# A mixer's decays: read as repeated rows and clamped by ScalarE, in place of products on TensorE

## The reference

```python
proj = einsum('bld,pd->blp', hidden_states, in_proj_w)
gate, hbc, dt = proj[..., :I], proj[..., I:I + CONV_DIM], proj[..., -H:]
xBC = silu(conv_bias + sum_k pad(hbc)[:, k:k + L, :] * conv_weight[:, k])
x, Bm, Cm = xBC[..., :I], xBC[..., I:I + GN], xBC[..., I + GN:]
dt_p = softplus(dt + dt_bias);  A = -exp(A_log);  dA = exp(dt_p * A)
# step over the tokens, per head:
state = state * dA_t + dtx_t * B_t;  y_t = state . C_t
y = y + x * D;  yn = (y * rsqrt(mean_group(y * y) + EPS)) * norm_weight * silu(gate)
out = einsum('bli,di->bld', yn, out_proj_w)
```

## Time and profile before

| what | value |
|---|---|
| median of 3 runs | 1298.97 us (1296.31 to 1299.89) |
| the profiled execution | 1300.67 us |
| its span | 1298.9 us |
| TensorE busy (PE) | 1230.5 us, 95% |
| VectorE busy (DVE) | 933.9 us, 72% |
| ScalarE busy (ACT) | 702.5 us, 54% |
| GpSimd busy (POOL) | 653.6 us, 50% |
| moved by DMA | 57.52 MB, mean 44 GB/s |

### The profile page before, as it was taken

The page is one execution under the profiler, slowest core; times in us unless marked ns, Lnnn a source line. Parts: engine busy times, 40 slices in busy tenths (PEclk is TensorE's granted clock), DMA queues, the critical chain, the costliest instruction groups (busy, mean ns, idle before and its releaser), DMA issues. The chain is left out here.

```text
span 1298.9 us, 22009 instructions
## 1 busy us (share of the span) xinstructions
PE 1230.5 (95%) x6680; PEld 968.9 (75%) x6690; DVE 933.9 (72%) x1735; ACT 702.5 (54%) x1056; POOL 653.6 (50%) x707
## 2 busy tenths in 40 slices
PE   5999999999999999999999999999679999889976
PEld 4777777787778778777778878777557777667754
DVE  5786778669667866966886696688567555479995
ACT  3676676567567666756766675665543333222210
POOL 5057546655655655565465556545653343433330
PEclk9999999999999999999999999999789999889996
DMA  5111021011102101110210110010103322211100
GB/s 178 46 50 34 2 67 34 19 34 49 33 1 66 33 17 33 50 32 1 66 32 17 33 58 24 5 34 2 41 17 115 97 90 83 93 49 48 45 16 25
DMA packets 44233, 57.52 MB, mean 44 GB/s; under 512 B 10117, under 2 KB 21159, under 8 KB 43929
## 3 DMA queue, kind: packets, MB, share of 16 engines
q1 hardware_dynamic: 44185, 56.92, 14.3%
HBM read 49.95 MB, written 6.96 MB: 44 GB/s over the span
## 5 line engine op out<-in xcount | busy, mean ns | idle before, releaser
L722 DVE SCALAR_TENSOR_TENSOR conv<-p_tile,conv_taps,conv 128x511 f32<-128x511 f32 x189 | 141.3, 748 | 51.4 <-ACT conv L583 36.4
L831 DVE TENSOR_TENSOR em<-em,p_gb 128x512 f32<-128x512 f32 x128 | 82.1, 683 | 69.6 <-ACT em L630 69.5
L527 POOL TENSOR_TENSOR squares<-squares 128x256 f32<-128x256 f32 x64 | 48.0, 750 | 132.5 <-ACT squares L656 132.5
L94 PE MATMUL p_tile<-xn_hi,wc_hi 128*128 128x512 f32 x252 | 110.8, 440 | 0.9 <-DVE halo L726 0.9
L656 ACT ACTIVATE squares<-y 128x512 f32<-128x512 f32 x64 | 40.4, 631 | 112.5 <-DVE y L867 111.5
L722 DVE SCALAR_TENSOR_TENSOR conv<-p_gate,conv_taps,conv 128x511 f32<-128x511 f32 (+2 forms) x90 | 67.0, 745 | 46.7 <-ACT conv L583 43.1
L94 PE MATMUL p_tile<-xn_lo,wc_hi 128*128 128x512 f32 x252 | 98.8, 392 | 0.0
L94 PE MATMUL p_d<-wr_hi,zt_hi 128*128 128x512 f32 x236 | 94.0, 398 | 1.5 <-ACT em L630 1.5
L94 PE MATMUL p_d<-wr_lo,zt_hi 128*128 128x512 f32 x236 | 93.1, 394 | 0.0
L495 POOL TENSOR_TENSOR x_w<-xs,head_g 128x512 f32<-128x512 f32 x56 | 58.4, 1043 | 68.7 <-ACT xs L624 63.6
L588 ACT ACTIVATE xbc<-conv 128x512 f32<-128x512 f32 x96 | 60.7, 632 | 59.7 <-DVE conv L730 37.4
(11 more groups left out here) (393 smaller groups left out, 3605.1 us busy)
## 6 DMA issues: line engine op xcount, KB each, us to landing
w_raw<-w SPq DMA_DIRECT2D x108, 256.0 KB, 2.7
q_words<-q SPq DMA_DIRECT2D x33, 256.0 KB, 2.7
h_ring<-h_lo_rows SPq DMA_DIRECT2D x6, 704.0 KB, 4.8
h_lo_rows<-h_rest SPq DMA_DIRECT2D x11, 256.0 KB, 2.1
x_res<-x SPq DMA_DIRECT2D x8, 256.0 KB, 4.1
out<-out_t SPq DMA_DIRECT2D x8, 256.0 KB, 2.0
h_lo_rows<-h_rest SPq DMA_DIRECT2D x11, 128.0 KB, 1.9
gate_second<-w SPq DMA_DIRECT2D x4, 256.0 KB, 5.0
```

The lines of the kernel that those rows point to most:

```text
L94: pe.matmul(out, lhs(k)[0], rhs(k)[n], start=(start and k == 0 and n == 0), stop=False)
L722: ve.scalar_tensor_tensor(out=conv[:, s, sh:], in0=p[:, 0:HALF - sh], scalar=conv_w[:, bass.ds(g, 1), j, tap], in1=conv[:, s, sh:], op0=AL ...
L831: ve.tensor_tensor(m, m, gm.unsqueeze(1).broadcast_to([P, HG // 2, P]), ALU.mult)\
```

## The change

TensorE's products L1085 and L1095 go, with the bf16 parts of cum, `d_lhs`, `d_rhs`, `head_rows` and their DMAs. In their place the start writes cum and exp(cum) to DRAM in float32, [chunk, head, token]. Per chunk one DMA reads the group's 8 rows of cum, 1024 columns, into all 128 partitions of em (`load_cum`), and two DMAs read each head's row of exp(cum) into that head's 64 partitions of e_cum (`load_e_cum`). ScalarE then makes relu(cum[s] - cum[t]) in place, per head, with cum[s] as a bias column from `cum_tok` (`decay_steps`, 8 activations of 128x128), and later exp of minus that; the clamp takes the mask's place, and the product with B and C stays masked. The exp of e_cum is done once, at the start.

```diff
+        def load_cum(g, c):
+            n = g * NC + c
+            wait(sp, s_intra, n - 1)
+            row = at(sp, g + c * G)
+            sp.dma_start(em[:, c % 2, :], cum_rows.rearrange("c (g h) t -> (c g) (h t)", g=G)[bass.ds(row, 1), :]
+                         .broadcast_to([P, HG * P])).then_inc(s_dl[c % 2], 16)
+        def load_e_cum(g, c):
+            wait(sp, s_t, g * (NC - 1) + c - 1)
+            row = at(sp, g + c * G)
+            own = e_rows.rearrange("c (g j a) t -> (c g) a j t", g=G, a=2)[bass.ds(row, 1)]
+            for a in range(2):
+                sp.dma_start(by_tile(e_cum[a * HD:(a + 1) * HD, :]),
+                             own[:, a, :, :].broadcast_to([HD, GW // P, P])).then_inc(s_ecl, 16)
...
         def group(g, last):
             for c in range(NC):
+                if c + 1 < NC:
+                    load_e_cum(g, c + 1)
                 if c + 2 < NC:
-                    load_d(g, c + 2)
+                    load_cum(g, c + 2)
...
+        def decay_steps(g, c):
+            act.wait_ge(s_dl[c % 2], 16 * (g * (NC // 2) + c // 2 + 1))
+            for h in range(HG):
+                steps = em[:, c % 2, h * P:(h + 1) * P]
+                made = act.activation(steps, steps, ACT.Relu, scale=-1.0, bias=cum_tok[:, c, bass.ds(g * HG + h, 1)])
+            made.then_inc(s_e, 1)
...
-                act.wait_ge(s_d, n + 1)
-                wait(act, s_intra, n - 1)
-                if last and c >= CH:
-                    act.activation(e_cum[:], p_in[:], ACT.Exp).then_inc(s_ec, 1)
-                for k, p in enumerate((p_d0, p_d1)):
-                    act.activation(em[:, c % 2, k * 512:(k + 1) * 512], p[:], ACT.Exp).then_inc(s_e, 1)
-                if c > 0 and not (last and c >= CH):
-                    act.activation(e_cum[:], p_in[:], ACT.Exp).then_inc(s_ec, 1)
+                act.wait_ge(s_e, 3 * n + 1)
+                for k in range(2):
+                    decay = em[:, c % 2, k * 512:(k + 1) * 512]
+                    act.activation(decay, decay, ACT.Exp, scale=-1.0).then_inc(s_e, 1)
...
+                if c < NC - 1:
+                    decay_steps(g, c + 1)
+                elif not last:
+                    decay_steps(g + 1, 0)
                 act.wait_ge(s_y, n + 1)
...
+        act.wait_ge(ln_st, NC + 3)
+        act.activation(t_ecum, t_cum, ACT.Exp).then_inc(dt_ac, 1)
         act.wait_ge(dt_tp, 3)
         act.activation(by_half(dtw_t), transposed(p_gb), ACT.Exp).then_inc(dt_ac, 1)
-        act.activation(by_half(etot_t), transposed(p_d0), ACT.Exp).then_inc(dt_ac, 1)
+        act.wait_ge(dt_tp, 4)
+        act.activation(by_half(etot_t), transposed(p_y), ACT.Exp).then_inc(dt_ac, 1)
...
                     wait(ve, s_sq, n)
                     wait(ve, s_z, n)
+                    ve.wait_ge(s_ecl, 32 * st)
                     ve.tensor_tensor(y[:], p_in[:], e_cum[:], ALU.mult).then_inc(s_t, 1)
...
-                pe.wait_ge(s_dl[c % 2], 32 * (g * (NC // 2) + c // 2 + 1))
-                if c > 0:
-                    wait(pe, s_t, g * (NC - 1) + c - 1)
-                    for j in range(GW // P):
-                        pe.matmul(p_in[:, j * P:(j + 1) * P], head_rows[:, j, :], d_lhs[:, c % 2, :],
-                                  start=True, stop=True)
-                wait(pe, s_e, 2 * n)
-                wait(pe, s_res, n - 2 if tail and c > CH else n - 1)
-                wait(pe, s_v, n - 1)
...
-                for k in rows_in(last, c - 1):
-                    pe.wait_ge(l2_lo, k + 1)
-                for k, p in enumerate((p_d0, p_d1)):
-                    mm = pe.matmul(p[:], d_lhs[:, c % 2, :], d_rhs[:, c % 2, k * 512:(k + 1) * 512],
-                                   start=True, stop=True)
-                mm.then_inc(s_d, 1)
...
                 if not first and not tail:
-                    pe.wait_ge(s_e, 2 * n + 1)
                     out_product(n - 1, out_bank(last, c))
-                    pe.wait_ge(s_e, 2 * (n + 1))
+                    wait(pe, s_v, n - 1)
                     sum_rows(n - 1, ss_bank(last, c))
...
             conv_tile(j, 0, j, 0, (p_tile, p_d1)[j % 2])
+            if j == 2:
+                pe.wait_ge(dt_ve, 12)
+                for b in range(CH):
+                    mm = pe.transpose(p_y[:, b * P:(b + 1) * P],
+                                      t_cum[:, (b + 1) * P - 1:(b + 1) * P].broadcast_to([P, P]), ident[:])
+                mm.then_inc(dt_tp, 1)
```

More of the change, by code:

```diff
@@ L172, in mixer @@
     gm = p_gb[:, 2 * P:3 * P]
[L176 removed]
+    cum_rows, e_rows = (nc.dram_tensor(k, [NC, H, P], F32, kind="Internal").ap() for k in ("cum_rows", "e_cum_rows"))
     w_rows = io["w"].rearrange("n p c -> (n p) c")
@@ L192, in mixer @@
         sem(f"l2_{k}") for k in ("st", "var", "rs", "xn", "tr", "hi", "lo"))
[L194 to L198, removed]
+    s_xt, s_gb, s_prj, s_gate, s_ss, s_out, s_inter, s_intra, s_stn = (
+        sem(f"pe_{k}") for k in ("xt", "gb", "prj", "gate", "ss", "out", "inter", "intra", "stn"))
+    s_xs, s_e, s_cin, s_xc, s_sg, s_zhi, s_sq, s_whi = (
+        sem(f"act_{k}") for k in ("xs", "e", "cin", "xc", "sg", "zhi", "sq", "whi"))
     s_head = sem("ve_head")
@@ L339, in mixer @@
     t_w = y[:]
-    t_parts = [x[:, 0:GW // 2].bitcast(BF16) for x in (x_dt, x_w, x_d)]
+    t_ecum = x_d[:]
     t_mask = squares[:, 0:GW // 2].bitcast(BF16)
@@ L398, in sync @@
             load_w(0, w)
-        for k in range(PART):
-            wait(sp, dt_ve, 12 + k)
+        for rows, made in ((cum_rows, (ln_st, NC + 3)), (e_rows, (dt_ac, 6))):
+            sp.wait_ge(*made)
             for a in range(2):
[L403 to L408, removed]
+                heads_a = (t_cum if rows is cum_rows else t_ecum)[a * H:(a + 1) * H, :]
+                sp.dma_start(rows[a * CH:(a + 1) * CH].rearrange("c h t -> h c t"),
+                             heads_a.rearrange("h (c t) -> h c t", t=P)).then_inc(s_parts, 16)
+        sp.wait_ge(s_parts, 16 * 4)
+        load_cum(0, 0)
+        sp.wait_ge(dt_tp, 4)
+        sp.wait_ge(dt_ve, 11)
+        load_cum(0, 1)
         def group(g, last):
             for c in range(NC):
+                if c + 1 < NC:
+                    load_e_cum(g, c + 1)
                 if c + 2 < NC:
-                    load_d(g, c + 2)
+                    load_cum(g, c + 2)
                 elif not last:
-                    load_d(g + 1, c + 2 - NC)
+                    load_cum(g + 1, c + 2 - NC)
                 if not last:
@@ L1038, in row_transpose @@
             if p_row[k] is p_d1:
-                pe.wait_ge(s_e, 2 * (n + 1))
+                wait(pe, l2_lo, {2: 1}.get(k, 0))
                 if k == NC - 2:
@@ L1110, in group @@
                     pe.wait_ge(s_stu, g * (NC - 1) + c)
-                    pe.wait_ge(s_ec, g * (NC - 1) + c)
+                    wait(pe, s_t, g * (NC - 1) + c - 1)
                     for j in range(GW // P):
@@ L1165, in tensor @@
         pe.wait_ge(dt_ve, 11)
-        for src, dst in ((t_dt, p_y), (t_rem, p_gb), (None, p_d0)):
+        for src, dst in ((t_dt, p_y), (t_rem, p_gb), (t_cum, p_d0)):
             for b in range(CH):
-                rows_c = src[:, b * P:(b + 1) * P] if src is not None \
-                    else t_cum[:, (b + 1) * P - 1:(b + 1) * P].broadcast_to([P, P])
-                mm = pe.transpose(dst[:, b * P:(b + 1) * P], rows_c, ident[:])
+                mm = pe.transpose(dst[:, b * P:(b + 1) * P], src[:, b * P:(b + 1) * P], ident[:])
             mm.then_inc(dt_tp, 1)
```

68 lines of the change are left out of this document (14 added, 54 removed).

## The result

| | before | the changed kernel |
|---|---|---|
| median | 1298.97 us | 1290.65 us (1289.21 to 1294.09, 5 runs) |
| ratio | | 0.9942, 95% interval 0.992 to 0.9965 |
| profiled execution, its span | 1300.67, 1298.9 | 1290.2, 1288.3 |
| PE / ACT busy | 1230.5 / 702.5 us | 1199.4 / 822.0 us |
| moved by DMA | 57.52 MB | 105.01 MB |

The account below looks back on a forecast made before the run. TensorE's own work was taken to set seven of eight groups. From 1300.67 us: -28.0 for seven groups, -1.6 and -5.0 in the last, +3.2 start, -1.7 from profile to median: 1268 us, range 1256 to 1289.

Parts of the forecast that it names:

- VectorE's work stays: VectorE in the loop: its 128 products with em and the taps remain; y times e_cum now waits for a DMA.
- The clamp's price: ScalarE, eight clamps per chunk: 0.30 us each from start to start, 2.4 us per chunk, bounds 0.2 and 0.39.
- Rival 1: ScalarE's clamps don't overlap, 0.39 us each, 0.72 us more per chunk: 1285 us in all; chance 0.17.
- Rival 3: The em loads come late, over 12.3 us each, so ScalarE waits at the clamps: slower than before; chance 0.08.
- rival 4: No change: the removed products fill time TensorE would wait anyhow, the start eats the rest: 1297 to 1301; chance 0.05.
- Chunk 0 to 1: Loop boundary where the clamps delay squares and the rounded z holds out_product: gives nothing, -0.1 us.
- Chunk 1 to 2: Loop boundary where the convolution tile waits 0.1 us for the gate's silu, clamps hidden: 0.56 us won.
- 0.2 to spare: Chunk 1 to 2, ScalarE: clamps and squares end at 543.2, ahead of the gate's silu at 543.39.
- Chunks 4 to 5 and 5 to 6: Loop boundaries where the convolution tile waits for the gate's silu to empty p_tile: 0.56 us won each.
- Chunks 2 to 3, 3 to 4, 6 to 7 and 7 to 0: Loop boundaries: the first three, with the bank free early, give 0.66 us each; 7 to 0 gives 0.44.
- The start: Before the loop: later exp of chunk totals +2.9, first clamps +1.5, out_product's em wait gives back 1.2; together +3.2 us.
- The tail: Last group, chunks 4 to 7: waits for p_d's bank and e_cum go; 5.0 us won, between 2 and 9.

Follow-up runs that it names:

- best2: Changed kernel, e_cum wait on TensorE, ScalarE's loop written out, chunk 1's clamps behind z's rounding, start's exp behind the tiles' copies: 1268.6 us, 0.9758.
- dve_unrolled: The changed kernel with VectorE's hardware loop over groups 1 to 6 written out, ScalarE's loop kept: 1281.53 us, ratio 0.9883.
- before_pad12: The kernel before with twelve unused one-column activations a chunk added on ScalarE in chunks 1 to 7 of the looped groups: 1299.81 us, 1.0003.

## Why the prediction was wrong

The terms of the sum come to -31.4 us, and -10.6 was measured in the profiled executions (spans 1298.9 and 1288.3). Term by term:

| term | forecast | measured |
|---|---|---|
| start (first heads' product 69.85 to 75.67, then 1.25 won at 0-1) | +3.2 | +4.6 |
| seven group ends and boundaries, jumps aside | -28.0 | -21.8 |
| jumps back, five | none | +12.1 |
| last group, to chunk 3 | -1.6 | -0.2 |
| last group, chunks 3 to 7 | -5.0 | -3.3 |
| behind it | 0 | -1.9 |

**The step that failed** is a missing one, the largest part of the 20.8 us between the two: the jump back stood in the sum at nothing, without a reason. The part on ScalarE priced each added instruction by its time on the engine, but nothing asked what longer bodies do to the loop's jump. "VectorE's work stays" was true of its work; the seven register instructions a turn that came with its new wait were not counted, and with them taken off VectorE its stall of 5.4 to 6.1 us is gone. In place of nothing the runs showed 12.1 us over five jumps. The second part is the term of the boundaries, 6.2 us too large, taken up below. With the jumps cured, the kernel runs at 1279 to 1280 us, inside the range though 11 to 12 above the forecast.

**The clamp's price was right.** A row of eight lasts 2.44 us, (2.44-0.39)/7 = 0.29 from start to start; 0.30 was taken. Rival 1 falls. The estimate of 0.41 us by the Trainium skill's budget (ScalarE: Activation LUTs, Rules for kernel authors) is near the 0.389 that one lasts, and too high for a row. Rival 3 falls too: em's loads land in 4.0 us where 5.4 was taken. So does rival 4: four of the eight boundaries give the whole time of the products that went.

**Chunk 0 to 1** went as written: out_product waits for zt_hi (0.42 us in this row, where the earlier trace rows had em), and the boundary gives 0.06 where -0.1 was forecast.

```profile
531.15 0.47 PE L91 MATMUL p_d<-wr_hi,zt_hi 128*128 128x512 f32 x1 [0.42 <-ACT zt_hi L592]
```

**Chunk 1 to 2 was mis-sized: 0.56 forecast, 0.02 measured.** ScalarE there, to hold against the earlier trace rows:

```profile
539.89 0.76 ACT L582 ACTIVATE conv<-p_gate,conv_taps 128x512 f32<-128x512 f32 x1
540.55 2.44 ACT L599 ACTIVATE em<-em,cum_tok 128x128 f32<-128x128 f32 x8
542.89 0.62 ACT L663 ACTIVATE squares<-y 128x512 f32<-128x512 f32 x1
543.41 0.58 ACT L622 ACTIVATE gate_second<-p_tile 128x512 f32<-128x512 f32 x1
...
544.04 0.50 PE L91 MATMUL p_tile<-xn_hi,wc_hi 128*128 128x512 f32 x1 [0.36 <-ACT gate_second L622]
```

The clamps end and squares starts at 542.89, so the silu at 543.41 is bound by ScalarE's own row of work. The "0.2 to spare" was taken with the copy-in as it stood before. Counted from chunk 1's heads' product (539.26 before, 538.83 now) the copy-in starts 1.06 us behind it where it was 0.26, because the silu ahead of it waits for VectorE's taps, and the gate's silu 4.58 where it was 4.13. I read that as the late rounding of z in chunk 0 carried on through VectorE (zt_lo at 531.37 there). best2, in which that rounding is ahead of the clamps, has 12.56 in place of 12.95 here, so 0.4 of the 0.54 missing come back; the two edits were not run apart.

**Chunks 4 to 5 and 5 to 6** gave 0.31 each where 0.56 was taken. The gate's silu is on time there, and TensorE's tile starts 0.22 us behind its end:

```profile
583.29 0.60 ACT L622 ACTIVATE gate_first<-p_tile 128x512 f32<-128x512 f32 x1 [0.23 <-PE p_tile L95]
...
584.11 0.49 PE L91 MATMUL p_tile<-xn_hi,wc_hi 128*128 128x512 f32 x1
```

In the rows of chunk 1 the silu ends at 543.99 and the tile starts at 544.04. The difference is in the code: these tiles belong to the next group, so behind the wait for the silu TensorE has two more waits, for that group's rounded weights, and register work for them. In the trace they stand between 583.93 and 584.11, one after another. The forecast took TensorE to start almost with the silu's end. **Chunks 2 to 3, 3 to 4, 6 to 7 and 7 to 0** gave 0.64, 0.64, 0.64 and, without a jump, 0.44, as forecast.

**The start** happened as described: ScalarE's exp of the chunk totals at 48.73 (49.2 forecast), tile 2's copy-in at 51.66 (52.0), and convolution tile 4 at 55.03 (55.4):

```profile
55.03 0.79 PE L91 MATMUL p_tile<-xn_hi,wc_hi 128*128 128x512 f32 x1 [3.58 <-DVE halo L738]
```

The 1.4 beyond the forecast is within what the start varies by: kernels with the same start as the changed one have their first heads' product between 74.40 and 76.37, and those with the start of the kernel before between 69.85 and 72.37.

**The tail** gave 3.3 in chunks 3 to 7, and part of that is luck. The wait for x_w came as forecast: in chunk 5 the product with x_w starts 6.04 us behind the heads' product ahead of it, where it was 8.34, so 2.3 us earlier of the 2.6 taken. But TensorE still stands idle there, for x_w now, and the whole moves with its granted clock. From chunk 4's heads' product to chunk 5's, in the kernel before:

```profile
923.90:938.50 14.60, 11.35 (x62) 8.29 (x61) 8.91 (x17) 7.03 (x13) 10.15 (x12) 0.77 0.20 59
```

By stretch between heads' products from chunk 3 to chunk 6, the changed kernel and then dve_unrolled:

```profile
899.00:919.20 20.20, 12.95 (x67) 9.97 (x67) 10.37 (x26) 10.56 (x21) 11.56 (x17) 0.75 0.17 53
919.20:930.20 11.00, 7.86 (x58) 6.27 (x56) 8.77 (x18) 8.66 (x20) 8.62 (x12) 1.00 0.31 78
930.20:942.20 12.00, 8.87 (x52) 6.96 (x51) 8.26 (x17) 6.93 (x17) 8.63 (x10) 0.86 0.63 168
```

```profile
887.00:907.60 20.60, 13.37 (x69) 10.21 (x68) 10.51 (x26) 10.62 (x21) 11.66 (x17) 0.75 0.17 52
907.60:921.20 13.60, 10.47 (x56) 7.96 (x55) 8.82 (x17) 8.58 (x20) 9.67 (x12) 0.75 0.26 69
921.20:934.40 13.20, 10.07 (x52) 7.54 (x51) 8.38 (x18) 6.95 (x17) 7.53 (x9) 0.74 0.56 146
```

With the stretch to chunk 7, the same instructions take 53.6 us in the one and 57.6 in the other: 4 us of tail hang on how long TensorE runs at the lower of its two levels (1.2 and 2.4 GHz) behind the same waits. Over all profiled executions chunks 3 to 7 take 53.4 to 58.2 us in the twelve kernels with the change and 55.1 to 58.6 in the seven without, so 3.3 is one draw, and what the tail gains at an equal clock isn't shown. The 1.9 us behind the mixer may be of the same kind: with the same code there, six of the kernels without the change take 337.5 to 337.8 us behind the last heads' product and the seventh, before_pad12, 335.2; the difference lies in the first 25 us, at a granted clock of 0.92 for 0.86. The kernels with the change all take 335.6 to 335.9. Why chunks 0 to 3 of the last group gave only 0.2 stays open.

## What to carry to other kernels

Where a change adds instructions inside a hardware loop, look at the time behind each branch, engine by engine, and at the instruction queue's packets per turn: where both loops were kept and neither stalled there were none, or two or three over the five jumps. The count of executed instructions, with the register work of waits and addresses, says what was added, but not whether it stalls: 358 didn't and 342 did. Two engines can stall at the same jump and hide each other, so curing one alone showed nothing on ScalarE and only a part on VectorE. The cures that worked here are a wait moved to an engine with room, operands that need no register, a loop written out, and the loop moved in the code; since the place decides, any later edit may bring the stall back. Re-price an edit that spends ScalarE's slack only after that, since behind a stall it costs more than it wins.

## What the hardware showed that was not expected

- ScalarE or VectorE went on 2.4 to 6.8 us behind a jump back or at once (0.22 to 0.34 us), with nothing between, and seven instructions in 379 on VectorE or a shift by 64 on ScalarE decided it. An engine that stalls brings about 25 more packets of 8 KB over the five jumps.
- TensorE executes over 700 instructions a turn, weight loads and register work counted and matmuls not, and went on 0.1 us behind each of its branches, in every kernel here.
- In the last group the granted clock was 0.75 or 1.00 over the same chunk in two kernels with the same instructions there, which moved 2.7 us in that one chunk.
